# Last chunk's inverse deviations on ScalarE and VectorE instead of GpSimd, and a pair's keys made ahead of shared products

## The reference

```python
x = x + _layernorm(_L0_attn_ref(_layernorm(x), ...))   # 16 heads of 8, relative position bias, softmax over 1024 keys
x = x + _layernorm(_L0_ffn_ref(_layernorm(x), ...))    # 64 experts, 8 per token out of 4 of 8 groups, plus a shared expert

def _layernorm(x, axis=-1, eps=1e-05):
    m = jnp.mean(x, axis=axis, keepdims=True)
    v = jnp.var(x, axis=axis, keepdims=True)
    return (x - m) / jnp.sqrt(v + eps)
```

## Time and profile before

| | us |
|---|---|
| median of 3 runs | 1121.36 (1118.37 to 1123.12) |
| the profiled execution | 1122.23 |
| its span | 1120.4 |
| busy: PE, DVE, ACT, POOL | 911.1, 816.9, 685.9, 555.9 |
| attention until | about 850 |
| tail of the routing | 850 to 943 |
| expert phase | 943 to about 1064 |
| closing phase | about 1064 to the end |

### The profile page before, as it was taken

The page is one execution under the profiler, slowest core; times in us unless marked ns, Lnnn a source line. Parts: engine busy times, 40 slices in busy tenths (PEclk is TensorE's granted clock), DMA queues, the critical chain, the costliest instruction groups (busy, mean ns, idle before and its releaser), DMA issues. The chain is left out here.

```text
span 1120.4 us, 16485 instructions
## 1 busy us (share of the span) xinstructions
PE 911.1 (81%) x5190; PEld 289.5 (26%) x5190; DVE 816.9 (73%) x1314; ACT 685.9 (61%) x1416; POOL 555.9 (50%) x729
## 2 busy tenths in 40 slices
PE   5657999999999999999999999999986541745076
PEld 3311222222222222222222222222212321534043
DVE  6787888889889988988988998898841540322057
ACT  5714777777787777778778777777884210333113
POOL 6780020124356455645735554563576754456425
PEclk9867999999999999999999999999998665666578
DMA  5893432012332222222223212000222003410097
GB/s 140 262 250 63 118 80 62 15 38 47 83 110 87 90 90 55 59 49 82 82 91 104 49 39 50 5 6 14 79 82 91 2 3 90 119 51 13 17 400 275
DMA packets 107181, 96.35 MB, mean 86 GB/s; under 512 B 51406, under 2 KB 86512, under 8 KB 105046
## 3 DMA queue, kind: packets, MB, share of 16 engines
q1 hardware_dynamic: 89846, 88.12, 26.7%
q0 software_dynamic: 14336, 4.25, 1.8%
q10 hardware_dynamic: 2912, 2.93, 1.2%
HBM read 49.36 MB, written 65.24 MB: 102 GB/s over the span
## 5 line engine op out<-in xcount | busy, mean ns | idle before, releaser
L269 DVE TENSOR_REDUCE half_max<-s_pair 128x2 f32<-128x1024 f32 x512 | 602.0, 1218 | 77.8 <-PE s_pair L258 73.2
L1423 ACT ACTIVATE probs<-st_bank 128x512 f32<-128x512 f32 x1024 | 544.1, 602 | 170.3 <-PE st_bank L1519 157.2
L1285 POOL DMA_INDIRECT table<-rows,keys_i x256 | 255.5, 998 | 180.7 <-PE pv_bank L1528 67.5
L1519 PE MATMUL st_bank<-q_stack,k_stack 98*128 98x512 bf16 (+1 forms) x1024 | 324.0, 387 | 13.0 <-ACT probs L1423 4.9
L1528 PE MATMUL pv_bank<-probs,values 128*9 128x512 f32 x2048 | 267.7, 595 | 3.1 <-ACT unit_out L1358 2.8
L258 PE MATMUL s_pair<-k_stack,q_stack 64*128 64x512 bf16 x1024 | 202.5, 395 | 28.7 <-DVE half_max L269 26.4
L258 PEld LDWEIGHTS s_pair<-k_stack,q_stack 64*128 64x128 bf16 x1024 | 49.2, 93 | 344.3 <-issue 197.4
L1519 PEld LDWEIGHTS st_bank<-q_stack,k_stack 98*128 98x128 bf16 (+1 forms) x1024 | 77.7, 97 | 171.4 <-issue 86.2
L1721 POOL DMA_INDIRECT results<-out,ids x64 | 62.2, 971 | 53.7 <-ACT out L1783 37.3
L1754 DVE TENSOR_TENSOR h<-s_pair,gsig 128x256 f32<-128x256 f32 x16 | 6.8, 425 | 71.3 <-ACT gsig L1775 53.1
L1174 POOL CAST shift<-minus_max 128x16 bf16<-128x16 f32 x32 | 6.4, 201 | 101.2 <-DVE minus_max L275 101.1
(11 more groups left out here) (253 smaller groups left out, 845.9 us busy)
## 6 DMA issues: line engine op xcount, KB each, us to landing
results<-zeros SPq DMA_DIRECT2D x8, 2048.0 KB
choices<-results SPq DMA_DIRECT2D x6, 2048.0 KB, 23.7
table<-blank SPq DMA_DIRECT2D x8, 772.0 KB, 7.3
probs<-table SPq DMA_DIRECT2D x16, 386.0 KB
q_stack<-q_image SPq DMA_DIRECT2D x96, 64.0 KB
k_stack<-k_image SPq DMA_DIRECT2D x96, 64.0 KB
k_image<-k_piece SPq DMA_DIRECT2D x16, 256.0 KB, 3.3
table<-rows,keys_i POOLq DMA_INDIRECT x256
```

The costliest lines, as they stand in the source:

```text
L269: nc.vector.tensor_reduce(halves[:, h:HG:SIDE_HEADS, tile, half], stacks.s_pair[slot % S_SLOTS][:].rearrange("p (s k) -> p s k", s=SIDES), ...
L1285: pool.indirect_dma_start(out=table, out_offset=bass.IndirectOffsetOnAxis(ap=keys_i[c % 2][:, pick:pick + 1], axis=0), in_=rows[c % 2][:, ...
L1423: A.activation(probs[:, s % P_SLOTS, :], st_bank[at % ST_BANKS][:], ACT.Exp).then_inc(bank_free, 1)
L1519: M(bank(at)[:], k_stack[g][own, tile // PER, h, tile % PER * P:(tile % PER + 1) * P], q_stack[g][own, half, h, :], start=True, stop=True) ...
```

## The change

The change has four parts, all in the tail:

1. GpSimd no longer makes the two inverses of the last chunk, and `LEFT_RUNS` is gone: its queue in the tail is scatters alone. For the other chunks it still makes them.
2. ScalarE takes the root of var + EPS (`root`), VectorE the reciprocal of that and one Newton step on it, and the shift (`last_inverse`). The root needs another function table. A trial activation on one column stands ahead of `copy_y` with the root and another, with the sigmoid, ahead of `norm_xf`.
3. On VectorE `pair_slots(v)` comes directly behind `choose_pair(v)`, ahead of the two `shared_h`.
4. `tile_keys` and `tile_weights` become one semaphore, `tile_rows`, so a scatter of chunk 7 waits three times instead of four. A constant (`eps`) is added to GpSimd's set-up in the first unit.

```diff
-LEFT_RUNS = (12, 4)
...
-        SETUP, BO_STEPS = 9, 10
+        SETUP, BO_STEPS = 10, 10
...
+            def last_inverse(mv, done, rstd, less, less_done, v):
+
+                dve.wait_ge(done, CHUNKS)
+                dve.wait_ge(less_x1_done, LAST)
+                then(V.tensor_scalar(veps[:], mv[:, :, 1], EPS, None, ALU.add))
+                dve.wait_ge(rooted, v + 1)
+                then(V.reciprocal(rstd[:], rstd[:]))
+                then(V.scalar_tensor_tensor(out=less[:], in0=rstd[:], scalar=-0.5, in1=rstd[:], op0=ALU.mult, op1=ALU.mult))
+                then(V.tensor_tensor(less[:], less[:], veps[:], ALU.mult))
+                then(V.scalar_tensor_tensor(out=rstd[:], in0=less[:], scalar=1.5, in1=rstd[:], op0=ALU.add, op1=ALU.mult))
+                V.scalar_tensor_tensor(out=less[:], in0=mv[:, :, 0], scalar=-1.0, in1=rstd[:], op0=ALU.mult, op1=ALU.mult).then_inc(less_done, 1)
...
             output_stats(LAST)
+            last_inverse(mv_y, var_y_done, rstd_y, less_y, less_y_done, 0)
             last_residual()
             residual_stats(LAST)
+            last_inverse(mv_x1, var_x1_done, rstd_x1, less_x1, less_x1_done, 1)
             for v in range(PER // PAIR):
                 choose_pair(v)
+                pair_slots(v)
                 shared_h(2 + 2 * v)
                 shared_h(3 + 2 * v)
-                pair_slots(v)
...
+                G.memset(eps[:], EPS).then_inc(setup_done, 1)
...
-                    pool.wait_ge(tile_keys, pick // TOPK // PAIR + 1)
-                    pool.wait_ge(tile_weights, pick // TOPK // PAIR + 1)
+
+                    pool.wait_ge(tile_rows, 2 * (pick // TOPK // PAIR + 1))
...
-            left = LEFT_AT
-            for run, inverse_of in zip(LEFT_RUNS, (output_norm, residual_norm)):
-                for pick in range(left, left + run):
-                    scatter(pick // picks, pick % picks)
-                inverse_of(LAST)
-                left += run
-            for pick in range(left, CHUNKS * picks):
+            for pick in range(LEFT_AT, CHUNKS * picks):
                 scatter(pick // picks, pick % picks)
...
+            def root(mv, done, rstd):
+                act.wait_ge(done, CHUNKS)
+                A.activation(rstd[:], mv[:, :, 1], ACT.Sqrt, bias=eps[:]).then_inc(rooted, 1)
+
...
             shared_gate(1)
+
+            act.wait_ge(setup_done, SETUP)
+            A.activation(trial[:], ones16[:, 0:1], ACT.Sqrt)
             copy_y(LAST)
+            root(mv_y, var_y_done, rstd_y)
             for t in range(PER):
                 norm_y(LAST, t)
             shared_keep(0)
             shared_keep(1)
+            root(mv_x1, var_x1_done, rstd_x1)
+            A.activation(trial[:], ones16[:, 0:1], ACT.Sigmoid)
             for t in range(PER):
                 norm_xf(LAST, t)
```

More of the change, by code:

```diff
@@ L752, in attend_and_route @@
         recip_done, normed_done = sem("recip_done"), sem("normed_done")
+        trial, eps = sb("trial", [P, 1]), sb("eps", [P, 1])
+        rooted = sem("rooted")
         var_y_done, less_y_done, y_normed = sem("var_y_done"), sem("less_y_done"), sem("y_normed")
@@ L762, in attend_and_route @@
         tile_turned, tile_xfT, tile_logits, tile_scored = sem("tile_turned"), sem("tile_xfT"), sem("tile_logits"), sem("tile_scored")
-        tile_chosen, tile_ranked, tile_ranks, tile_weights, tile_keys = (sem(f"tile_{name}") for name in ("chosen", "ranked", "ranks", "weights", "keys"))
+        tile_chosen, tile_ranked, tile_ranks, tile_rows = (sem(f"tile_{name}") for name in ("chosen", "ranked", "ranks", "rows"))
         s_sig, s_h = [probs[:, v, :] for v in range(2)], [probs[:, 2 + v, :] for v in range(2)]
@@ L1093, in choose_pair @@
                 V.scalar_tensor_tensor(out=weights, in0=chosen[:, mine, :], scalar=NOT_CHOSEN, in1=weights,
-                                       op0=ALU.add, op1=ALU.add).then_inc(tile_weights, 1)
+                                       op0=ALU.add, op1=ALU.add).then_inc(tile_rows, 1)
             def pair_slots(v):
@@ L1107, in pair_slots @@
                 then(ins)
-                V.tensor_scalar(keys_i[LAST % 2][:, of8], keys[:, of8], -1.0, None, ALU.add).then_inc(tile_keys, 1)
+                V.tensor_scalar(keys_i[LAST % 2][:, of8], keys[:, of8], -1.0, None, ALU.add).then_inc(tile_rows, 1)
+            def last_inverse(mv, done, rstd, less, less_done, v):
[8 more added lines that the diff above has]
+                V.scalar_tensor_tensor(out=less[:], in0=mv[:, :, 0], scalar=-1.0, in1=rstd[:], op0=ALU.mult, op1=ALU.mult).then_inc(less_done, 1)
             sum_reciprocals(LAST)
```

## The result

| | before | after |
|---|---|---|
| median, us (20 runs each) | 1121.72 (1118.37 to 1124.91) | 1126.51 (1121.78 to 1133.02) |
| the profiled execution | 1122.23 | 1121.78 |
| its span | 1120.4 | 1120.0 |

The ratio of the times is 1.0042 [1.0028, 1.0056]: 4.8 us slower, where 10.5 us faster was forecast. That is outside the predicted range, and inside the 0.5% that the prediction called no change.

What follows compares the result with a forecast made beforehand. GpSimd's queue of 60 tail scatters was taken as the bound, ending 14.0 us above its pace; pair 1's scatters ending 10.5 us earlier gave 1122.2 - 10.5 - 0.9 = 1110.8 us as a median, range 1106.5 to 1118.

Steps and rivals of the forecast that it cites:

- scatters alone don't make it: Tail: pair 0 was chosen beside scatters at full pace (7.64 us), taken as evidence against handshake slowness moving with the scatters.
- the stretch follows pair 1: Rival: slow handshakes from 894 to 919 move along with pair 1; only 3.4 us won; 0.24 shared with gain given back.
- keys 0: Tail, VectorE: pair 0's keys, made directly after its choosing, ready at 887.3, before GpSimd arrives at 887.9.
- the hidden shared products: Tail: shared_h(4) to (7) after pair 1's keys cost nothing, with cover from 901 to 929.
- gain is given back: Rival: expert phase meets one more wait and loses the 10.5 us, median 1122; 0.24 shared with the full stretch.
- activations of the rows: Tail, ScalarE: norm_xf of x1 starts at 874.2 instead of 878.46, 4.2 us earlier, set by table load and trial.
- reordering's part: Tail, VectorE: keys ahead of shared products give about 2 of the 6.6 us by which pair 0's scatters start earlier.
- nothing in the change removes its cause: Tail: pair 0's slow scatter block, 23.45 us, may stay, so 10.5 was taken from 10.0 to 13.0 us.
- The unowned gap of 1.93 us: GpSimd, chunk 6's scatters: one gap without owner; if it stays they end at 888.5 rather than 886.9; 887.9 taken.
- The load: ScalarE: the root's table load, 1.28 us, and trial end at 864.5, hidden before copy_y at 865.31, 0.8 us to spare.
- VectorE's new steps beside scatters: Tail: if ten new small steps each held a scatter up by 0.17, 1.7 us lost and the sum 8.8; not counted.
- Slower by two waits in the expert phase: Rival: the expert phase meets two more waits, 23.5 us against 10.5 won, median 1134; chance 0.05.

Runs made afterwards that it cites:

- inv_only: Changed kernel with the keys back behind the two shared products, so only the inverses' move remains; 1125.81 us, ratio to before 1.0053.
- wait_once: Changed kernel whose tail scatters wait on semaphores only where the value is new, once per pair or tile; 1127.78 us, ratio to before 1.0074.
- after_again: The changed kernel unchanged, run again on a chip where semaphore updates come promptly; ratio to before 0.9962.
- before_again: The kernel before unchanged, traced on a chip where semaphore updates come promptly; 1 run, last scatter ends 84.95 us from the end of attention.
- rests: Changed kernel with four dependent dummy powers on GpSimd after tail scatters 12 and 16, on a chip with prompt semaphore updates; ratio to before 1.0038.

## Why the prediction was wrong, by its steps

**What failed: "scatters alone don't make it".** The rival "the stretch follows pair 1" was given a small weight because pair 0 was chosen beside scatters too, at full pace. The experiments show the opposite: without the tail's scatters there is no late signal, with them there was one in every trace of a late chip. In the step's own terms, the sum had GpSimd arrive at pair 0 at 37.6 us from the end of attention, keys 0 at 37.0 and the last scatter's end at 81.0. In the profiled execution of after GpSimd was through with chunk 6 at 40.7, keys 0 were there at 44.9, GpSimd waited 4.97 us for them, and the last scatter ended at 86.8: 4.7 us won at this place instead of 10.5.

Pair 0 was quick in before, and its choosing began right behind a rest of GpSimd's queue (876 to 879). The rests were in the rows, as gaps and inverses; I read them as lost time only. Removing them was what the change is for; that on a late chip this also removes what limits the lateness is my reading of inv_only, which lost 6.3 us by it. It is read from where the signals arrive, which speaks both ways, and wasn't tried by an experiment on such a chip. It stays open, too, whether density of scatters or a plain count of them since the last rest is what matters.

**What failed second: the hidden shared products.** The step put shared_h(4) to (7) at nothing, with cover from 901 to 929. It counted VectorE's time, not the handshakes TensorE, ScalarE and VectorE make for each chunk. Each of these is a signal that can be late: ScalarE idles 13.90 and 14.16 us before two copies of after. The cover is gone, and what shows is 953.42 - 947.7 = 5.7 us in the profiled execution, which is what the scatters had won (4.7) and a little more. In wait_once it is 107.7 against 98.6 + 6.8 = 105.4. In inv_only the scatters themselves end late (96.6), and 6.8 behind them come the experts. The rival "gain is given back" was nearest in size (1122 forecast for it, 1126.5 measured) but by luck, since it put the place wrongly: not in the expert phase, which took 104.2 us against 108.9, but in the same tail.

**What held on prompt chips**, where before has neither slow block nor late signal; times from the end of attention:

| step | predicted | after_again |
|---|---|---|
| activations of the rows, earlier than before by | 4.2 | 4.4 (23.7 against 28.2) |
| keys 0 | 37.0 | 38.0 |
| keys 1 | 49.0 to 51.0 | 50.0 |
| last scatter ends | 81.0 (78.5 to 81.5) | 80.0 |
| reordering's part | about 2 | 2.6 |
| 28 scatters of chunk 6 end | 36.6 to 38.2 | 36.3 |

So the new chain was sized rightly to a microsecond. One of its terms was too small: from 871.33 on TensorE's shared_up(2) and (3) took 6.70 us in after_again, at a granted clock of 0.55, where the rows of before had 5.31, at 0.69, so the first transpose came at 27.0 instead of 25.8, and the keys 1.0 late with it. That the scatters end within 1.0 us of the forecast is in part luck: the sum had no wait for keys 0 (2.57 measured), and it had 20.5 to 23.45 us for pair 0's scatters and 20.4 for pair 1's, where the 32 took 41.1 in all. And the gain was counted against a kernel before whose last scatter ended at 91.5; of those 14.0 us above the floor, 84.95 - 77.5 = 7.5 are there on a prompt chip. Of these, 5.0 were won at the last scatter and 4.5 in the medians (1093.26 against 1097.78). The rest was the late signals' own, and "nothing in the change removes its cause" was said of the slow block only, not of the wait of 3.71 and not of pair 1's choosing.

**Smaller steps.** *The unowned gap of 1.93 us.* In before_again it stands at the same place (869.83, second scatter behind the first inverse), in rests behind the first rest (1.98), and in after_again there is none. It goes with the rest before it, and so with the inverses; I had let it stay. On the late chip after has three such gaps without a rest (1.85, 0.89 and 2.38 us between 871 and 878), which the trace doesn't explain either. *The load.* Hidden as the step said: load and trial end at 868.40, 14.3 us from the end of attention (14.2 predicted), and ScalarE then waits 0.73 for the projection. The Trainium skill, "ScalarE: Activation LUTs", section "What ACT_TABLE_LOAD costs", would add a drain of 1.38 us; the load starts 0.01 us after the second gate's end and the trial 0.02 us after the load's, so this trace disagrees. *VectorE's new steps beside scatters.* The Trainium skill, "GPSIMD Engine Reference", section "Specifications", says that GpSimd shares its SBUF interfaces with VectorE; my estimate beside it was up to 1.7 us. The 28 scatters of chunk 6 follow each other by (886.14 - 851.32) / 27 = 1.290 us in after_again, and the 44 behind the second rest in before_again by 1.284: 0.2 us in all, so no run here shows it. *Slower by two waits in the expert phase:* not seen; that phase is 91.1 against 90.7 us on prompt chips.

## What to carry to other kernels

If a trace has "remote" waits of several us beside indirect DMAs, compare the time of the semaphore's update with the end of the instruction that makes it, and don't count on a calm stretch of the kernel before to stay calm when the DMAs around it move closer together. Don't call work with many handshakes hidden because it has time enough. Follow every engine's queue to the end of the stage, not only the one that ended last before. And time such a change on more than one chip, and more than once: this one came out 0.4% faster where signals were prompt and 0.4% slower where they were late.

## What the hardware showed that I had not expected

- Signals that are late by far more than any instruction: 8.5 and 21.6 us from the end of TensorE's matmuls to ScalarE's copy with scatters, 0.04 without. It is not every engine's: in the four traces with tail scatters on late chips, TensorE's updates come up to 23.8 us behind the end of their instruction and VectorE's up to 4.5, also those that VectorE itself waits for between its dependent steps (1.1 us in before, against 0.01 elsewhere), but none of ScalarE's more than 0.01. In the expert phase there, only TensorE's are late (up to 11.0). The Trainium skill, "Perfetto Trace Analysis", section "Per-engine timelines", says that a record leaves out the way of a semaphore's update to the other engines; this is where such time would hide. These traces show it all the same, by the time of the update (930.30 and 945.05).
- All four traces of kernels with tail scatters on late chips have it (before, after, inv_only, wait_once), none of the 12 on prompt chips has: the largest delay of an update is 0.05 us there in the tail and 0.03 in the expert phase. The kernel before is 23 us slower on late chips by the medians; its two traces differ by 28.0, of which 6.6 lie in the tail (91.5 against 84.95 for the last scatter), 18.2 in the expert phase (108.9 against 90.7) and 3.1 before the end of attention. What sets the two conditions apart is not known.
- 128 rows by an indirect DMA hold GpSimd for 1.28 us and a direct DMA of the same size for 0.54. Of the gap of 0.30, redundant waits are no measurable part.
